# A fused attention and FFN layer: the order of two elementwise products chosen per chunk, with later step offsets and more buffers

## What is computed

```python
x = x + attn_a(_layernorm(x), ...)   # channel attention: 8 heads of 16, l2 norm over the 512 positions
x = x + ffn(_layernorm(x), ...)
x = x + attn_b(_layernorm(x), ...)   # one head of 128, piecewise scaled scores (sps_pro), softmax
x = x + ffn(_layernorm(x), ...)      # same weights again

def ffn(h):                           # E = 8 experts of I = 336
    probs = softmax(h @ router_w.T)
    a_h = gelu(h @ actor_w1.T + actor_b1)
    k = argmax(clip(a_h @ actor_w2.T + actor_b2, -30, 30)) + 1
    scores = where(rank(probs) < k, probs, 0)
    for e in range(E):
        g, u = h @ gate_w[e].T, h @ up_w[e].T
        out += scores[..., e:e+1] * ((silu(g) * u) @ down_w[e].T)
```

## Time and profile before

| | |
|---|---|
| median of 3 runs | 533.03 us (529.68 to 537.04) |
| the profiled execution | 532.75 us, span 531.0 us |
| PE busy | 495.8 us, 93% |
| DVE busy | 348.6 us, 66% |
| Pool busy | 291.2 us, 55% |
| ACT busy | 239.2 us, 45% |

### The profile page before, as it was taken

How to read it: one execution, slowest core, us unless ns; L and a number is a source line. 1 busy time by engine, 2 the same in 40 slices (tenths; PEclk the granted TensorE clock), 3 DMA queues, 4 the chain that set the end, 5 groups by cost and what they waited for, 6 DMA issues and landing times.

```text
span 531.0 us, 6553 instructions
## 1 busy us (share of the span) xinstructions
PE 495.8 (93%) x2128; PEld 349.3 (66%) x2128; DVE 348.6 (66%) x769; ACT 239.2 (45%) x399; POOL 291.2 (55%) x280
## 2 busy tenths in 40 slices
PE   6797989999996997998989999899998999999996
PEld 6665756776664665766757777577775677666663
DVE  3649483775699797568785699956989354653332
ACT  3386326246622735423836248462383523523221
POOL 4346794238578092734565357553564544655553
PEclk9999999999999998999999999989999899999999
DMA  8600000000000000000000000000000000000000
GB/s 248 200 0 2 0 2 0 1 0 2 1 0 1 0 1 1 0 2 0 2 0 1 0 0 2 0 1 1 21 1 0 1 21 0 1 2 20 0 1 20
DMA packets 7917, 7.38 MB, mean 14 GB/s; under 512 B 716, under 2 KB 7756, under 8 KB 7884
## 3 DMA queue, kind: packets, MB, share of 16 engines
q1 hardware_dynamic: 7884, 6.97, 4.3%
HBM read 5.91 MB, written 1.05 MB: 13 GB/s over the span
## 4 chain that ended last, share of the span: by engine, by line
PE 63%; DVE 16%; issue 4%; ACT 2%; POOL 1%; DVEq 0%; POOLq 0%; ACTq 0%
PE bank L1085 20%; PE bank L949 12%; PE bank L951 11%; PE bank L950 11%; PE bank L1136 3%; DVE t L883 2%; DVE xn L735 2%; PE bank L1124 1%; DVE mk L909 1%; PE bank L1053 1%; DVE mk L908 1%; DVE mk L913 1%; DVE gt L843 1%; DVE mk L912 1%; DVE ge L837 1%
## 5 line engine op out<-in xcount | busy, mean ns | idle before, releaser
L530 POOL TENSOR_TENSOR t<-t,sl 128x512 f32<-128x512 f32 x105 | 136.3, 1303 | 123.0 <-DVE t L883 120.5
L633 ACT ACTIVATE sl<-bank 128x512 f32<-128x512 f32 x168 | 99.9, 597 | 182.8 <-PE bank L951 147.6
L1085 PE MATMUL bank<-t,WD 128*128 128x512 f32 x336 | 168.1, 595 | 0.8 <-ACT YT L639 0.8
L883 DVE TENSOR_TENSOR t<-bank,sbc 128x512 f32<-128x512 f32 x105 | 71.9, 685 | 77.0 <-PE bank L951 76.8
L949 PE MATMUL bank<-xhF,WGh 128*128 128x512 f32 x168 | 100.5, 598 | 2.7 <-ACT sl L633 2.0
L530 POOL TENSOR_TENSOR t<-t,sbc 128x512 f32<-128x512 f32 x63 | 81.6, 1326 | 6.0 <-ACT sbc L627 5.9
L1085 PEld LDWEIGHTS bank<-t,WD 128*128 128x128 f32 x336 | 63.7, 190 | 27.8 <-issue 13.8
L949 PE MATMUL bank<-xhF,WUh 128*128 128x512 f32 x168 | 68.4, 407 | 7.7 <-DVE t L883 7.7
L883 DVE TENSOR_TENSOR t<-bank,sl 128x512 f32<-128x512 f32 x63 | 42.7, 684 | 43.7 <-ACT sl L633 25.8
L951 PE MATMUL bank<-xhF,WUl 128*128 128x512 f32 x168 | 67.1, 399 | 0.0
L951 PE MATMUL bank<-xhF,WGl 128*128 128x512 f32 x168 | 67.0, 399 | 0.0
(11 more groups left out here) (180 smaller groups left out, 688.3 us busy)
## 6 DMA issues: line engine op xcount, KB each, us to landing
stage<-in_gate SPq DMA_DIRECT2D x7, 192.0 KB, 6.1
stage<-in_up SPq DMA_DIRECT2D x7, 192.0 KB, 6.3
WD<-in_down SPq DMA_DIRECT2D x7, 192.0 KB, 6.2
X<-in_x SPq DMA_DIRECT2D x4, 256.0 KB, 5.5
out<-X SPq DMA_DIRECT2D x4, 256.0 KB, 2.3
raw<-in_small SPq DMA_DIRECT2D x1, 388.0 KB, 4.6
raw<-in_small SPq DMA_DIRECT2D x1, 192.0 KB, 2.7
rows<-in_row SPq DMA_DIRECT2D x1, 136.0 KB
```

Source lines behind the costliest of these rows:

```text
L530: pool.tensor_tensor(t2[k % NT2][:, :], t2[k % NT2][:, :], by[:, :], ALU.mult).then_inc(a_done, 1)
L633: act.activation(sl[k % NSL][:, :], bank[k % 2][:, :], ACT.Silu).then_inc(silu_done, 1)
L883: dve.tensor_tensor(t2[k % NT2][:, :], bank[2 + k % 2][:, :], by[:, :], ALU.mult).then_inc(t2_done, 1)
L1085: pe.matmul(OACC[:, :], WD[:, c, :], t2[k % NT2][:, :], start=(c == 0), stop=(c == CH - 1))\
```

## The change

The choice between the two orders is made per chunk: `plan()` marks chunk k as `routed_last` (DVE takes `sl`, Pool `sbc`) when, at the time DVE's product is issued, the block's sbc has not been issued or Pool's product of the chunk before has not (`len(um_end) < k`). All waits follow this set. A block may begin as soon as xl has been issued. NSL goes from 2 to 3 and NT2 from 16 to 20. A_STEPS, A1_STEPS, B_STEPS and F_STEPS get later offsets, F1_STEPS is dropped for F_STEPS, and the last A thread starts at 25 instead of 24.

```diff
--- before.py
+++ after.py
@@ -47,7 +47,7 @@
 
 X10, X25, X85, X95 = (-2.1972245773362196, -1.0986122886681098, 1.7346010553881064, 2.9444389791664403)
 AFTER_POOL = 1.6
-NSL, NT2 = 2, 16
+NSL, NT2 = 3, 20
 WCH = 3
 WCOLS = WCH * P
 NPIECES = 3 * CH // WCH
@@ -75,28 +75,24 @@
            ("y", 0), ("warm", 4), ("wp", 3), ("stats", "F", 0), ("xn", "A", 1), ("ag", 1), ("xn", "F", 0), ("wp", 4),
            ("xT", "F", 0), ("xT", "A", 1), ("xl", "F", 0), ("ar", 1), ("swl", 0)]
 WARM = (12, 2, 4, 7, 10)
-A_STEPS = [(0, "stats"), (1, "xn"), (3, "ag"), (4, "xT"), (5, "ar"), (7, "asim"), (8, "ass"), (9, "ascale"),
-           (11, "asT"), (12, "amax"), (13, "aexp"), (14, "awo"), (16, "am"), (17, "am2"), (19, "y")]
-A1_STEPS = [(2, "asim"), (3, "ass"), (4, "ascale"), (6, "asT"), (7, "amax"), (8, "aexp"), (9, "awo"),
-            (11, "am"), (12, "am2"), (14, "y")]
+A_STEPS = [(0, "stats"), (1, "xn"), (4, "ag"), (5, "xT"), (6, "ar"), (8, "asim"), (9, "ass"), (10, "ascale"),
+           (12, "asT"), (13, "amax"), (14, "aexp"), (15, "awo"), (17, "am"), (19, "am2"), (21, "y")]
+A1_STEPS = [(2, "asim"), (3, "ass"), (4, "ascale"), (7, "asT"), (8, "amax"), (9, "aexp"), (10, "awo"),
+            (12, "am"), (13, "am2"), (15, "y")]
 F0_STEPS = [(0, "route"), (1, "inner", 0), (2, "rexp"), (3, "inner", 1), (3, "rsum"), (5, "rrank"), (5, "tanh"),
             (6, "gelu"), (8, "act"), (8, "actk"), (11, "sbc")]
-F1_STEPS = [(0, "stats"), (0, "xn"), (3, "xT"), (4, "xl"), (6, "route"), (7, "rexp"), (7, "inner", 0),
-            (9, "inner", 1), (9, "rsum"), (11, "rrank"), (11, "tanh"), (11, "gelu"), (13, "act"),
-            (13, "actk"), (16, "sbc")]
-ROUTED_LATE = (0, 1, 2)
-B_STEPS = [(0, "stats"), (2, "xn"), (4, "xT"), (4, "xl"), (6, "bqk", 0), (7, "bqk", 1), (7, "bqkl", 0),
-           (7, "bqkl", 1), (10, "bs", 0), (10, "bsp", 0, 0), (11, "bsp", 0, 1), (13, "bsp", 0, 2),
+F_STEPS = [(0, "stats"), (1, "xn"), (4, "xT"), (5, "xl"), (7, "route"), (8, "rexp"), (8, "inner", 0),
+           (10, "rsum"), (11, "inner", 1), (12, "rrank"), (13, "tanh"), (14, "gelu"), (16, "act"),
+           (17, "actk"), (20, "sbc")]
+B_STEPS = [(0, "stats"), (2, "xn"), (4, "xT"), (4, "xl"), (7, "bqk", 0), (8, "bqk", 1), (8, "bqkl", 0),
+           (8, "bqkl", 1), (11, "bs", 0), (10, "bsp", 0, 0), (11, "bsp", 0, 1), (13, "bsp", 0, 2),
            (15, "bs", 1), (14, "bsp", 0, 3), (15, "bsp", 1, 0), (16, "bv"), (15, "bsp", 1, 1),
            (17, "bsp", 1, 2), (18, "bs", 2), (18, "bsp", 1, 3), (19, "bsp", 2, 0), (19, "bexp", 0),
            (19, "bexp", 1), (20, "bsp", 2, 1), (21, "bsp", 2, 2), (22, "bs", 3), (25, "bsp", 2, 3),
            (22, "bsp", 3, 0), (25, "bsp", 3, 1), (26, "bsp", 3, 2), (27, "bsp", 3, 3), (28, "bexp", 2),
            (27, "bexp", 3), (30, "bpT", 0), (31, "bpT", 1), (30, "bpT", 2),
            (32, "bpT", 3), (34, "bo", 0), (34, "bo", 1), (35, "bo", 2), (35, "bo", 3), (35, "byx")]
-F_STEPS = [(0, "stats"), (1, "xn"), (3, "xT"), (4, "xl"), (6, "route"), (7, "rexp"), (7, "inner", 0),
-           (10, "inner", 1), (9, "rsum"), (12, "rrank"), (12, "tanh"), (12, "gelu"), (14, "act"),
-           (14, "actk"), (18, "sbc")]
-A_STARTS = (6, 24)
+A_STARTS = (6, 25)
 B_STARTS = (29, 48, 67, 90)
 M_START = 7
 SHIFTS = 1
@@ -161,7 +157,7 @@
 
 
     last = CH * 2 * NB
-    threads = [thread("F", n, {0: F0_STEPS, 1: F1_STEPS}.get(n, F_STEPS), CH * n - F_AHEAD if n else 0) for n in range(2 * NB)]
+    threads = [thread("F", n, F_STEPS if n else F0_STEPS, CH * n - F_AHEAD if n else 0) for n in range(2 * NB)]
     threads += [[CH * (n + 1) + 3, [(0, ("yT", n))], 0] for n in range(2 * NB - 1)]
     threads += [[M_START, [(0, ("wbT", 0)), (2, ("wvp", 0)), (4, ("bvp", 0))], 0]]
     threads += [thread("B", b, B_STEPS, B_STARTS[b]) for b in range(NB)]
@@ -172,6 +168,7 @@
     debt = [0.0, 0.0]
     pool_free = [0.0]
     um_end, downs = [], [0]
+    routed_last = set()
 
     def ready(s):
         if not all(v in done or v[1] < 0 for v in needs(s)):
@@ -220,11 +217,12 @@
         assert ready(s), s
         add(s)
     while k < last - 1:
-        n = (k + 1) // CH
-        if (k + 1) % CH or (("xl", "F", n) if n in ROUTED_LATE else ("sbc", n)) in done:
+        if (k + 1) % CH or ("xl", "F", (k + 1) // CH) in done:
             k += 1
             add(("gu", k))
             assert k < NT2 or ("down", k - NT2) in done
+            if ("sbc", k // CH) not in done or len(um_end) < k:
+                routed_last.add(k)
             add(("uk", k))
         else:
             for th in threads:
@@ -255,11 +253,11 @@
         k += 1
         products(k, 2)
     add(("yT", 2 * NB - 1))
-    return steps, order
+    return steps, order, routed_last
 
 
 def build(nc, x_d, small_d, gate_d, up_d, down_d, w2_d, cols_d, rows_d, out_d):
-    steps, norm_no = plan()
+    steps, norm_no, routed_last = plan()
     turn_of = {}
     turns = 0
     for s in steps:
@@ -520,7 +518,7 @@
                     k = s[1]
                     n = k // CH
                     pool.wait_ge(t2_done, k + 1)
-                    if n in ROUTED_LATE:
+                    if k in routed_last:
                         if k % CH == 0:
                             wait_free(pool, turn_of["sbc", n])
                         by = sbc[n % 2]
@@ -623,13 +621,13 @@
                     t = turn_of[s]
                     wait_full(act, t)
                     if n >= 2:
-                        act.wait_ge(a_done if n - 2 in ROUTED_LATE else t2_done, CH * (n - 1))
+                        act.wait_ge(a_done, CH * (n - 1))
                     act.activation(sbc[n % 2][:, :], m_bank(t)[:, :], ACT.Copy).then_inc(n_free(t), 1)
                 if kind == "gu":
                     k = s[1]
                     act.wait_ge(g_full, k + 1)
                     if k >= NSL:
-                        act.wait_ge(t2_done if (k - NSL) // CH in ROUTED_LATE else a_done, k - NSL + 1)
+                        act.wait_ge(t2_done if k - NSL in routed_last else a_done, k - NSL + 1)
                     act.activation(sl[k % NSL][:, :], bank[k % 2][:, :], ACT.Silu).then_inc(silu_done, 1)
                 if kind == "down" and s[1] % CH == CH - 1:
                     n = s[1] // CH
@@ -871,11 +869,11 @@
                     k = s[1]
                     n = k // CH
                     dve.wait_ge(u_full, k + 1)
-                    if n in ROUTED_LATE:
+                    if k in routed_last:
                         dve.wait_ge(silu_done, k + 1)
                         by = sl[k % NSL]
                     else:
-                        if k % CH == 0:
+                        if k % CH == 0 or k - 1 in routed_last:
                             wait_free(dve, turn_of["sbc", n])
                         by = sbc[n % 2]
                     if k >= NT2:
```

## The result

The changed kernel takes 573.84 us (median of 4 runs, 573.05 to 574.35) against 535.03 us before (4 runs, 529.68 to 537.18): a ratio of 1.074, with a 95% interval of 1.065 to 1.083. It is slower by 39 us, where 8 us less were forecast.

A forecast was written before the change was run, and what follows sets the result against it. PE, busy 93% of the 531.0 us span, was taken as the bound, so only its idle time and slow clock could change. Removed 10.6 us, added 2.8, net 7.8: 525 us, range 511 to 541.

The forecast's parts named there:

- the 1.9 us of the term: Order per chunk and three silu buffers: PE stalls at 239.28 (0.78) and 248.01 (1.09) go, 1.9 us removed.
- The terms of the longer lags: Steps of A, B and F moved later, so that PE's named waits for xn, gelu, xlS and others go.
- ag's 2.47 us at 50.58: Stream A's ag, one chunk later after xn: 2.3 us of this PE wait removed, 0.2 stays.
- act's 0.86 us: F's act on PE behind gelu: three such waits go, 2.6 us removed, bound 0.
- bqk's 2.78 us: PE's wait for xlS at 202.51, bqk one chunk later: only 0.7 us removed, bounds 0 and 2.8.
- The wait of 1.27 us before xT of block 1: F block 1's xn a step after its stats, xT one later: the wait at 73.73 goes, 1.3 us removed.
- the 1.3 us foreseen: Block 1's first gate matmul waits for a ScalarE copy and DVE subtraction: 1.3 us added, 0 to 3.2.
- bs and the first two bsp steps fall in one step now ... so nothing: B's mask steps: five more DVE instructions at once, four times; 0 us, bound 1.13 us four times.
- the 1.5 us for Pool's catching up: Pool clearing backlogs after blocks begin before their sbc, slowing DVE: 1.5 us added, bounds 0 and 26.
- The signs that the prediction named for this case: Slower xn and masks in blocks 4 to 6, DVE time well above 348.6, PE waits for t above 7.7 us.
- The fourth case: Pool's catching up slows DVE in first ten chunks of blocks 2 to 6, 3.8 us a stretch; chance 17%.
- one of three falls was counted as a gain of 1.8 us: PE's clock falls near 203, 346 and 411 us: one goes with its stall, 1.8 us removed, bounds 0 and 5.4.

The follow-up runs named there:

- e3: Changed kernel's order per chunk, block starts at xl and larger buffers, with all step tables and A_STARTS of before: 533.05 us (0.997).
- e12: Order per chunk with the step tables of before, only gelu, act and actk of blocks 2 to 7 one chunk later: 533.37 us (0.997).
- e17: Order per chunk with the step tables of before, only B_STEPS new: 536.35 us (1.001).
- e1: Changed kernel with B_STEPS of before: 563.49 us (1.054).
- e2: Changed kernel with F1_STEPS and F_STEPS of before: 540.55 us (1.011).
- e7: Changed kernel with F1_STEPS of before for block 1 alone: 555.40 us (1.041).
- e16: Changed kernel with A_STEPS, A1_STEPS and A_STARTS of before: 552.21 us (1.032).
- e18: Order per chunk with the step tables of before, only F's steps new (F1_STEPS dropped): 558.88 us, four runs from 549.16 to 561.45.
- e9: Changed kernel with each Pool product cut into two instructions of 256 columns: 545.79 us (1.024).
- e15: Kernel before with each Pool product cut into two instructions of 256 columns, nothing else: 522.62 us (0.979).
- e13: Changed kernel with each Pool product cut into four instructions of 128 columns: 527.55 us (0.988).
- e5: Kernel before with Pool's product cut from 512 to 16 columns, most of the second product left out: 509.96 us (0.955).
- e6: Changed kernel with Pool's product cut from 512 to 16 columns, most of the second product left out: 516.94 us (0.969).
- e14: Order per chunk with the step tables of before, each Pool product in four instructions of 128 columns: 517.79 us (0.969).

## Why the prediction was wrong

The order per chunk and the third silu buffer were read rightly: both orders cost the same, ScalarE's waits for Pool are gone, DVE takes the silu in 143 chunks (100 to 130 were expected), and the whole mechanism with old offsets is a gain of 1.4 to 2 us (e3). That this is the 1.9 us of the term is in part luck: e3 holds the rest of the mechanism too, and its trace still has the wait for YT (0.69 us at 241.31, for the 0.78 at 239.28); only the 1.09 us at 248.01 has gone.

The terms of the longer lags failed as gains. Each named wait did go, and these came back at a neighbouring instruction: ag's 2.47 us at 50.58 as 2.28 us of an up product at 50.98; act's 0.86 us as 1.23 us of an up product in e12; bqk's 2.78 us as 2.72 us of an up product at 207.46 in e17, where only B's table is new. The prediction used this argument for bqk alone ("the next up product would have waited") and should have used it wherever DVE was named. The wait of 1.27 us before xT of block 1 went, and the first gate matmul of block 1 waited 1.41 us for xlF, near the 1.3 us foreseen; but asT beside it grew from 0.86 to 2.70 us, with a stretch of lower clock behind it.

The first step that failed is "bs and the first two bsp steps fall in one step now ... so nothing". It gave the five no price and took PE's slack of two chunks, 4.6 us at its 2.3 us a chunk, to cover them. It did not price them at Pool's pace, though the earlier trace rows had shown that for xn: five mask instructions took 7.1 us (145.14 to 152.23). And it did not name what is queued behind them on DVE: awo, and through it am on PE, 8.1 us. e1 and e17 size it, together with bqk, which stands in the same table: 10 us beside the other offsets, nothing alone.

The second failure, and the largest, is the 1.5 us for Pool's catching up, chosen "near the low end" of 0 to 26. With 32 us of the loss gone once Pool's products are thin, this was the main term, and its upper bound was too low as well. The signs that the prediction named for this case all came: DVE is busy for 369.9 us instead of 348.6, the mean xn is 764 ns instead of 636, and PE waits 27.2 us for t instead of 7.7. The fourth case had the mechanism (chance 0.17, 550 us) but not the place. It looked for it at the starts of blocks 2 to 6, caused by the new order and early starts; e3 shows that these cost nothing with old offsets. Most of it is in blocks 2 and 3, where F's and A's offsets delay Pool until its run lies on rsum, the masks and awo (e2, e7, e16, e18). The prediction had seen that block 1's sbc comes four chunks later, and used it for buffers and not for what DVE does at that time.

The third is the sign of the clock: one of three falls was counted as a gain of 1.8 us; instead the stretches at 1.2 GHz grew from 10.2 to 47.8 us, and PE's busy time by 15.2 us. In the changed kernel each of the eight stalls of PE of 2.7 us or more has or shares such a stretch, which began during the stall or less than 0.5 us behind it (the two stalls at 213 and 220 us share one). It is no rule: in the kernel before, the stall of 3.22 us at 167.22 had none (clock 1.00 in the earlier trace rows).

On the Trainium skill ("SBUF — State Buffer", SBUF: two separate sides): its rule of an exclusive lock for a whole instruction agrees with masks of 1.4 us beside products of 1.3. The prediction read it as a wait for one instruction; the rows of e9, e18, e15 and e13 show 13.5, 12.4, 7.2 and 6.3 us.

What stays open: why one operation is held for many Pool instructions in e9, e13, e15 and e18, while in the changed kernel each of a dozen operations got in after one product; and the 7 us between e5 and e6, of which about 6 are idle time of PE (19.1 us against 12.7 from 20 us on). They may be the offsets by themselves, with no Pool in the way; no run tells. How much of e2's, e7's and e16's share is a longer run and how much a worse overlap was not separated.

## What to carry to other kernels

Where VectorE and GpSimd both work on SBUF, price each VectorE instruction that the trace shows stretched at the length of the GpSimd instruction beside it, know that it can be the whole run, and look first at what is queued behind it; a schedule moved by one chunk can turn a free step into a stall of PE. Cut GpSimd's elementwise work into short instructions before tuning lags: quarters took 15 us off here (e14 against e3) at the price of 88 us more work on an engine that had room, and made the kernel far less sensitive to its offsets (from 41 to 10 us between the two sets). Quarters did not end the long holds (6.3 us in e13). A removed wait counts as a gain only if the engine named in it is idle soon after.

## What the runs showed of the hardware

- A VectorE operation can be held through many GpSimd instructions in a row: 13.5 us through 18 of 0.7 us (e9), 12.4 us through ten of about 1.3 us (e18), 7.2 us through ten of 0.7 us (e15). Others, in the same kernels, waited for one.
- GpSimd's product of 128x512 takes 1.29 us at its median, of 128x256 0.74, of 128x128 0.46, of 128x16 0.22 us: by a line through these, a fixed part near 0.2 us (an estimate), so four pieces take 1.84 us for 1.29.
- With thin products the same 769 VectorE instructions take 288 us in the changed kernel and 292 in the one before, with full ones 370 and 349.
